# A Flamingo-style eight-stage kernel: unread TensorE products at six stage borders

## The reference

```python
x = x + tanh(g_xattn[0]) * L0_xattn(layernorm(x), ctx, ...)   # 32 heads of 8, ALiBi, banded masks
x = x + tanh(g_ffn[0])   * L0_ffn(layernorm(x), ...)          # 8 experts, best 2 of them, SwiGLU
x = x + tanh(g_xattn[1]) * L1_xattn(layernorm(x), ctx, ctx, gamma)
x = x + tanh(g_ffn[1])   * L1_ffn(layernorm(x), ...)          # 8 experts, dense weights
x = x + tanh(g_xattn[2]) * L2_xattn(layernorm(x), ctx, mask, ...)   # 16 heads, int8-like linears
x = x + tanh(g_ffn[2])   * L2_ffn(layernorm(x), factors, bias)
x = x + tanh(g_xattn[3]) * L3_xattn(layernorm(x), ctx, ctx)   # sigmoid attention
x = x + tanh(g_ffn[3])   * L3_ffn(layernorm(x), ...)          # shared and routed experts
```

## Time and profile before

| | |
|---|---|
| time, median of 3 runs | 1362.57 us (1351.86, 1362.57, 1577.53) |
| time of the profiled execution | 1366.6 us |
| its span, first to last instruction | 1364.8 us |
| mean granted TensorE clock | 0.921 of full speed |
| TensorE busy | 1095.8 us, 80%, 11717 matmuls |
| VectorE busy | 856.8 us, 63% |
| ScalarE busy | 543.2 us, 40% |
| GpSimd busy | 507.7 us, 37% |
| chain that ended last | PE 52%, DVE 19%, issue 10%, DMA 5%, ACT 5%, POOL 3% |

### The profile page before, as it was taken

How to read it: one execution, slowest core, us unless ns; L and a number is a source line. 1 busy time by engine, 2 the same in 40 slices (tenths; PEclk the granted TensorE clock), 3 DMA queues, 4 the chain that set the end, 5 groups by cost and what they waited for, 6 DMA issues and landing times.

```text
span 1364.8 us, 32895 instructions
## 1 busy us (share of the span) xinstructions
PE 1095.8 (80%) x11717; PEld 842.2 (62%) x11717; DVE 856.8 (63%) x2361; ACT 543.2 (40%) x1049; POOL 507.7 (37%) x1023
## 2 busy tenths in 40 slices
PE   4889889783784788887899799999756588879888
PEld 2667666562673344445666576667534478778888
DVE  3656566665454789867666577777655655545465
ACT  2455555454552467661100132323213633236433
POOL 2444455545884888511000111111322225410252
PEclk8899998997897699998999899999868988879999
DMA  5332322501675455421000100000012601124331
GB/s 187 110 110 79 112 89 94 176 18 43 198 214 161 123 141 145 118 67 62 1 0 0 32 21 19 20 19 15 0 39 75 189 7 47 51 90 155 114 97 62
DMA packets 105784, 112.61 MB, mean 83 GB/s; under 512 B 12548, under 2 KB 95636, under 8 KB 104892
## 3 DMA queue, kind: packets, MB, share of 16 engines
q1 hardware_dynamic: 96732, 88.47, 20.8%
q0 software_dynamic: 8064, 22.06, 5.3%
q10 hardware_dynamic: 864, 0.43, 0.1%
HBM read 66.07 MB, written 44.84 MB: 81 GB/s over the span
## 4 chain that ended last, share of the span: by engine, by line
PE 52%; DVE 19%; issue 10%; DMA 5%; ACT 5%; POOL 3%; another core or an unknown queue 3%; SPq 2%; DVEq 1%; ACTq 0%; POOLq 0%
PE psum L2630 5%; DMA PT<-xs 4%; PE psum L1080 3%; DVE mx L850 2%; DVE mx L2288 2%; PE psum L1656 2%; PE psum L1658 2%; PE psum L1657 2%; PE psum L2385 2%; PE psum L1135 2%; PE psum L1063 2%; PE psum L1043 1%; DVE mx L2522 1%; PE psum L1012 1%
## 5 line engine op out<-in xcount | busy, mean ns | idle before, releaser
L753 POOL TENSOR_SCALAR veps<-mv 128x1 f32<-128x1 f32 x112 | 27.2, 243 | 495.8 <-DVE mv L740 325.4
L850 DVE TENSOR_REDUCE mx<-psum 128x6 f32<-128x960 f32 (+3 forms) x80 | 80.7, 1009 | 78.1 <-PE psum L1048 58.4
L731 POOL DMA_INDIRECT got<-ys,rows_y x64 | 64.7, 1011 | 126.3 <-DMA ys<-yt 97.8
L937 ACT ACTIVATE PT<-psum 128x1024 f32<-128x1024 f32 x64 | 65.6, 1025 | 77.9 <-PE psum L1068 77.8
L2288 DVE TENSOR_REDUCE mx<-psum 128x4 f32<-128x1024 f32 x64 | 77.0, 1206 | 21.6 <-PE psum L2359 21.6
L2328 ACT ACTIVATE PT<-psum 128x1024 f32<-128x1024 f32 x64 | 65.6, 1025 | 36.4 <-PE psum L2370 35.1
L1656 PE MATMUL psum<-xnTh,w7h 128*128 128x256 f32 x256 | 77.3, 302 | 1.7 <-issue 1.7
L2630 PE MATMUL psum<-mskp,ident_r 128*128 128x512 f32 x256 | 71.4, 415 | 7.7 <-DVE mx L2522 6.4
L2099 DVE SCALAR_TENSOR_TENSOR x<-psum,cw,x 128x256 f32 (+1 forms) x128 | 53.1, 478 | 36.2 <-PE psum L2047 35.9
L1657 PE MATMUL psum<-xnTl,w7h 128*128 128x256 f32 x256 | 75.1, 293 | 0.3 <-issue 0.3
L1658 PE MATMUL psum<-xnTh,w7l 128*128 128x256 f32 x256 | 75.0, 293 | 0.3 <-issue 0.3
(11 more groups left out here) (412 smaller groups left out, 3435.4 us busy)
## 6 DMA issues: line engine op xcount, KB each, us to landing
xs<-qpad SPq DMA_DIRECT2D x17, 1024.0 KB, 5.2
PT<-xs SPq DMA_DIRECT2D x78, 128.0 KB, 2.1
ys<-yt SPq DMA_DIRECT2D x78, 128.0 KB, 2.2
ctxT<-in_ctxT SPq DMA_DIRECT2D x48, 128.0 KB
ext<-qscr SPq DMA_DIRECT2D x96, 64.0 KB
w_raw<-in_w SPq DMA_DIRECT2D x16, 384.0 KB, 3.5
arena<-in_w SPq DMA_DIRECT2D x4, 1280.0 KB, 10.1
q_parts<-kscr SPq DMA_DIRECT2D x66, 64.0 KB
```

What stands on the lines that cost most here:

```text
L731: pool.indirect_dma_start(out=dst[:, t % 4, k], out_offset=None, in_=ys[:], in_offset=bass.IndirectOffsetOnAxis(ap=rows_y[:, t, k:k + 1], ...
L850: V.tensor_reduce(mx0[:, u0:u0 + m].rearrange("p j e -> p e j"), src, axis=AX.X, op=ALU.max, negate=True).then_inc(F("mx").sem, 1)
L937: A.activation(PT[:, 1024 * r:1024 * (r + 1)], bank(6, 2), ACT.Exp).then_inc(F("p").sem, 1)
```

## The change

A helper `fill(o, n)` writes `n` matmuls: the unit matrix `identb` as weights, and as moving operand the same matrix read four times over, so 512 columns each, with `start=True, stop=True` into one bank. No instruction reads what they write, and they wait for nothing of their own. The table `FILL` puts them ahead of `stage_over` at the borders to stage 2 (72 of them, bank 4), 3 and 4 (26 each, bank 0), 6 (14, bank 0) and 7 (18, bank 2). A sixth place is in `tiles_pe` for stage 1: 32 of them in bank 4, between the wait for `w1_low` and the first tile's transposes. That makes 188 matmuls and as many weight loads. Nothing is removed.

```diff
+        FILL = {2: (4, 72), 3: (0, 26), 4: (0, 26), 6: (0, 14), 7: (2, 18)}
+
+        def fill(o, n):
+            for k in range(n):
+                nc.tensor.matmul(o, identb[:], identb[:].unsqueeze(1).to_broadcast([128, 4, 128]), start=True, stop=True)
...
             load_units(0)
             if L.st == 1:
                 pe.wait_ge(w1_low, TOP_E)
+                fill(bank(4), 32)
...
                 if 0 < s < n_stages:
+                    if s in FILL:
+                        fill(bank(FILL[s][0]), FILL[s][1])
                     stage_over(pe, s)
```

## The result

| | before | changed |
|---|---|---|
| median of the runs beside each other, us | 1359.4 | 1365.7 |
| ratio of the times, 95% interval | | 1.0067 (1.0049 to 1.0086) |
| the profiled execution's own time, us | 1366.6 | 1364.2 |
| its span, us | 1364.8 | 1362.3 |
| PE busy, us (instructions) | 1095.8 (11717) | 1124.3 (11905) |

The changed kernel is about 9 us slower (0.0067 x 1359.4), with a higher mean clock. The ratio is one of means over the fast executions; two of the fifteen of the kernel before, at 1577.5 and 5497.3 us, are not in it, and the plain medians differ by 6.4 us. The two profiled executions say -2.4 us, since single executions scatter by more than the whole change.

A forecast was written before the change was run, and what follows sets the result against it. TensorE carries about half the chain, VectorE, DMA and GpSimd the rest; stages start at 1.2 GHz after idling. 11.5 + 1.8 - 1.3 - 1.7 - 0.6 - 2.2 = +7.5 us, so median 1370 us, range 1354 to 1385.

The forecast's parts named there:

- rival B: Start of stage 2: the products keep the clock at 2.4 GHz into the stage; 4.5 us come off, 1365.6 us; chance 0.05.
- main term: Border to stage 2: the 72 products delay the late weights and VectorE behind them, +11.5 us.
- stage 2: Border: 72 products at 0.231 us delay the late weights; beyond VectorE's reserve first scores come later, +11.5 us (10.3 to 13.2).
- stage 1: Border: 32 products, part slow, make the first tile 4.3 us late; a faster start returns at most 2.6; +1.8 us.
- stage 6: Border: 14 products fit the idle time and warm the start; VectorE's norms pace the stage, so only -0.6 us.
- stage 7: Border: 18 products fit; transposes -0.4, router -0.9, first twelve up products about -1.1, less 0.2 for a wait: -2.2 us.
- Rival A: Border to stage 2: the 72 cost nothing, late weights are caught up before the first scores; -4.0 us, 1358.6; chance 0.10.
- Rival C: All borders: added products do not raise the clock and run at 0.43 us each; +48.9 us, 1411 us; chance 0.03.
- Stage 3: Border: 26 products fit the idle time; only faster transposes and router count, as TensorE then waits for VectorE; -1.3 us.
- Stage 4: Border: 26 products fit; the first sequence speeds up from 7.35 to the second's 5.63 us; -1.7 us, bound 3.1.

## Why the prediction was right or wrong

**The sum.** It forecast +7.5 us; measured were +9 and +7.3. The forecast of 1370 stands against 1365.7, since the kernel before itself had its median at 1359.4 in these runs. 1365.7 is also the time of rival B (1365.6), by chance: its mechanism did not happen, as is told below. The main term was right by its mechanism. That the sum came out so well besides is luck, since errors of both signs met in it, as the last column shows:

| term | forecast, us | by time | by the profiles |
|---|---|---|---|
| stage 2 | +11.5 | +10.8, +12.4 | +10.4 |
| stage 1 | +1.8 | +1.5 | -0.6 |
| stages 3 and 4 | -3.0 | -3.6 | -4.4 |
| stage 6 | -0.6 | +1.7 | +2.3 |
| stage 7 | -2.2 | -0.3 | -1.2 up to the tiles on two chips, +0.3 on the third |

The times of single parts have intervals of some 2 us to each side. They add up to +10.1 to +11.7, against +7.3 and +9. That rest is within these intervals; that the -0.3 comes from the one chip where stage 7 keeps none of its gain may be a part of it.

**Stage 2: right, and the one that decides.** Each step holds in the profile: the products are in front of the late weights, VectorE's L1295 waits 17.9 us (some 18 forecast), the wait for the gathered rows is used up, and GpSimd gives its 0.7 back. Only the price of one product was a little high, 0.231 for a measured 0.217. The Trainium skill's figure for isolated products (TensorE: Matmul & The Clock Gate, Back-to-back issue gap), 0.216 us, was the better one: the rows with 72 (0.218) and with 144 products (0.217) both agree with it, and the 10.4 us estimated from it for this term is what the border measured. Its rule that matmuls stay in program order (same page, Part 2) agrees too: with 144 products L1295 waits 33.46 us, and with the 72 behind the weights 3.09.

**Rival A** (the 72 are caught up) fell: the border grew by 10.4 us. It holds for 16 of them, which is the same reserve read from the other side. **Rival B** (the clock is kept into stage 2) fell twice: the stretch is at 0.51, and with the products right ahead of the scores stage 2 became 1.5 us shorter and not 4.5, which the time doesn't show. **Rival C** (0.43 us each) fell with 0.218 us. At stage 1, too, the 9.0 to 9.8 us for 32 products (six profiles) are near the forecast 9.9, part slow and part fast.

**Stage 1: right in its mechanism, its size open.** The first tile was 3.7 us late (4.3 forecast), and the tiles gave back 4.3 us by the mean of the profiles, more than the 2.6 that half of the slow stretch allows. That mean mixes chips: the net of wait and tiles is -1.4 us on one and +1.6 on another, each from few profiles that scatter by as much. The kernel with only the 32 is 1.5 us slower by its time, on the second of these chips, with an interval that reaches no difference. Whether this term is a small loss or nothing can't be told.

**Stage 3** gave 1.4 us (130.1 against 131.5 in the means of seven profiles each), as forecast with 1.3. The bound by VectorE is in the rows: the rest of the faster clock turned into the 1.93 us wait for `xn`. That the two numbers are so close is in part luck. Up to the seventh router five of the seven profiles keep 1.3 us (95.6 to 95.7 us against 96.9 to 97.0 in all seven without products), one keeps 0.9, and one (the kernel without the 72 and the 14) is 0.3 us late, because there the clock fell again 12 us into the stage: the second transposes took 1.12 us instead of 0.66. The last pair then takes either 16.6 us or 18.1, in profiles of both kinds (four and two of them have 16.6). In all eight with 18.1 the clock falls towards its end (0.56 to 0.76 over the last 3 us of it, or 15 to 18 us behind the seventh router), and in all six with 16.6 it stays at 1.00. Such a fall costs 1.6 us, more than the products give here.

**Stage 4: a term mis-sized.** It gave 3.0 us (233.4 against 236.4, seven profiles each), close to the bound of 3.1 and not 1.7. In the pair of profiles shown the first sequence became 2.2 us shorter, to 5.17, which is below the 5.63 of the second that it was compared with, because other waits stand in that one. But the 7.35 us of the earlier trace rows are the longest of the seven profiles without products (mean 7.0), so that the start gave 1.9 us in the mean, and comparing it with the second sequence was nearly right. What the forecast left out is the end: the step from the fifteenth scores to the sixteenth is 18.1 us in the mean with the products and 18.9 without, and another 0.4 us come behind it. Why the end of the stage is shorter was not traced.

**Stage 6: the step failed, in its sign.** It took "VectorE's norms pace this stage" as a reason for a small gain, and did not ask what a faster TensorE waits for next. That is the load of `cnat`. The third sequence's scores come 1.2 us earlier (4.4 us into the stage instead of 5.6), but the fourth's stand behind the load (wait of 3.24 us for the DMA) and come at 9.5 us, or 9.6 without the products. By then TensorE of the changed kernel has had 5.08 us of work in 9.3, the granted clock is 0.54, and the scores take 2.05 us for 1.10. The five profiles with the products all show this and the nine without all show the contrary: the products don't remove the slow part, they move it from 2 us into the stage to 9. (The first sequence's scores are fast in seven of the nine without any products (1.10 to 1.20 us); the kernel before of the earlier trace rows is one of the two others, so there was less to gain than it shows.) At the sixth sequence the five are still 0.5 us ahead (16.7 against 17.2 in the means), at the seventh 0.8 behind (21.5 against 20.6). At the end the five have 56.4 to 58.8 us (mean 58.0), the nine 55.0 to 58.5 (mean 55.8). Two of the nine, at 57.5 and 58.5, are as long as the five; their clock fell too, from some 13 us into the stage on. So the exchange is shown, and that it costs something by the seventh sequence; that it makes the whole kernel slower is likely, not shown, since the +1.7 us of the kernel with the 14 alone has an interval that just reaches zero. Why the clock falls is open. Idle time alone does not explain it: in the kernel with only the 72 TensorE is busy 3.96 of 7.00 us and then 2.36 of 5.00, and the clock stays at 1.00.

**Stage 7: the step failed.** Transposes and router did become faster as forecast (1.3 us by the second router). But the further 0.9 us for the up products is not there: the clock was back at 0.57 within 4.2 us. And the forecast took a gain at the start for a gain at the end. On two chips the 1.3 us last up to the tiles, 92 us into the stage; on the third, where TensorE has gaps between, they don't, and the time of the kernel with only the 18 shows nothing.

## What to carry to other kernels

Filler products for the clock are free only for the work behind them in TensorE's own list. Before putting any in, go through everything that stands behind them there, ask which engine waits for each, and count as free only that engine's reserve: here 3.8 us for VectorE (and some 0.6 of GpSimd's behind it), although TensorE itself had 19 idle. Then ask of the warm start how it goes on: it paid most where TensorE is busy nearly all of the slow stretch behind it (stage 4, 6.28 of 6.30 us: a gain of 3.0), about half of what it saved where TensorE must wait for VectorE next (stage 3: 1.3), and not at all, or worse, where TensorE must wait for a load next and then finds its clock low (stage 6). A gain at the start of a stage lasted on the chip where TensorE then had no gaps, and not on the one where it had (stage 7).

## What the runs showed of the hardware that was not expected

A start at 2.4 GHz doesn't last by itself. The granted clock was back at 0.54 to 0.57 after 9.3 us in stage 6 and 4.2 us in stage 7, the second time while TensorE was busy without a gap; it had been busy for 3.21 of the 4.20 us ahead of that. A slower start (0.81 over 9.0 us) was followed by a clock of 1.00 in stage 6. The Trainium skill (TensorE: Matmul & The Clock Gate, A second HAM failure mode: psum-queue depth-cycling) tells of a kernel whose clock went up and down because TensorE was idle for short times between groups of matmuls. The rows of stage 6 (5.08 busy of 9.30 us, then 0.54) are like it, but other rows of that stage speak against gaps as the whole cause (2.36 busy of 5.00 us at 1.00); no run here shows that gaps are the cause in stage 7. The mean clock of the execution rose from 0.921 to 0.94, while the time rose too. In stage 3 the clock falls some 110 us into the stage in eight of the fourteen profiles, with products or without, and costs 1.6 us where it does.

The same kernel differs between chips by more than this change: the kernel before took 1324, 1324 and 1356 us on three of them. One part of this is the first part of stage 7, up to its tiles, 91.7 to 93.1 us on two chips and 107 to 108 on the third; why is not known.
